# Placing each stage of the maxima and of the rest by table in a hand-ordered attention kernel

## What is computed

```python
# layer 0, per batch: attention over all 1024 tokens, 4 heads of 16
x_ln = layernorm(x) ; q, k, v = split(x_ln @ qkv_w)
attn = softmax(q k^T * scale) ; x = x + proj(attn v)
x = x + fc2(gelu(fc1(layernorm2(x))))
# layer 1, per batch: 8 heads of 64, each token sees the 32 tokens up to it
t = ln(tokens(x)) ; q, k, v = t Wq, t Wk, t Wv
t = tokens(x) + softmax_over_window(q . k_window) v_window @ Wu + bu
# then over all batches
Wx = ln(t) W ; Wx = batchnorm(Wx) ; y_t = sigmoid(Wx_t + y_{t-1} V^T)
result = t + y
```

## Time and profile before

| | us |
|---|---|
| three runs | 541.43, 546.31, 546.99 (median 546.31) |
| profiled execution | 541.36 |
| its span in the trace | 539.4 |
| PE busy | 461.1 |
| DVE busy | 328.0 |
| ACT busy | 291.6 |

### The profile page before, as it was taken

How to read it: one execution, slowest core, us unless ns; L and a number is a source line. 1 busy time by engine, 2 the same in 40 slices (tenths; PEclk the granted TensorE clock), 3 DMA queues, 4 the chain that set the end, 5 groups by cost and what they waited for, 6 DMA issues and landing times.

```text
span 539.4 us, 7934 instructions
## 1 busy us (share of the span) xinstructions
PE 461.1 (85%) x3257; PEld 178.3 (33%) x3257; DVE 328.0 (61%) x605; ACT 291.6 (54%) x499; POOL 12.9 (2%) x15
## 2 busy tenths in 40 slices
PE   7886889988989798787998987889998879995884
PEld 2442322222234332232233322222243323542583
DVE  3696868789748653689568654696332644514414
ACT  3442665755674365564873574648855655172242
POOL 9000000000000000000000000000000000000000
PEclk9896998989999999999999999999999998997897
DMA  8100180006300000017000000000000000000003
GB/s 295 28 1 2 41 136 1 1 1 121 56 2 1 1 1 1 1 33 144 0 2 1 1 1 2 0 0 1 2 2 1 1 0 1 2 1 1 1 1 79
DMA packets 6196, 13.09 MB, mean 24 GB/s; under 512 B 1296, under 2 KB 3600, under 8 KB 6032
## 3 DMA queue, kind: packets, MB, share of 16 engines
q1 hardware_dynamic: 6160, 12.58, 10.4%
HBM read 9.07 MB, written 3.41 MB: 23 GB/s over the span
## 4 chain that ended last, share of the span: by engine, by line
PE 66%; DVE 21%; ACT 8%; issue 3%; DMA 1%; SPq 1%; DVEq 0%; ACTq 0%
DVE part_max L1156 8%; PE O L725 8%; PE R L773 5%; PE T L690 4%; PE T L710 4%; PE R L621 3%; PE R L710 3%; PE R L882 3%; PE R L629 3%; PE R L690 3%; PE R L843 3%; PE R L870 2%; PE T L600 2%; PE R L857 2%; DVE zs L1267 2%
## 5 line engine op out<-in xcount | busy, mean ns | idle before, releaser
L1156 DVE TENSOR_REDUCE part_max<-T 128x1 f32<-128x512 f32 x170 | 112.0, 682 | 29.5 <-PE T L690 29.4
L1016 ACT ACTIVATE probs<-T 128x512 f32<-128x512 f32 x150 | 85.9, 597 | 41.2 <-PE T L710 41.0
L1016 ACT ACTIVATE probs<-R 128x512 f32<-128x512 f32 x106 | 62.0, 597 | 57.9 <-PE R L710 57.6
L690 PE MATMUL T<-KX,QX 96*128 96x512 bf16 x170 | 63.6, 395 | 9.7 <-DVE part_max L1156 8.3
L725 PE MATMUL O<-probs,VT 128*32 128x512 f32 x512 | 68.6, 611 | 1.1 <-ACT probs L1016 1.1
L1156 DVE TENSOR_REDUCE part_max<-R 128x1 f32<-128x512 f32 x86 | 57.4, 681 | 11.8 <-PE R L690 11.7
L710 PE MATMUL T<-QX,KX 99*128 99x512 bf16 x150 | 54.7, 389 | 7.5 <-DMA QX<-mx_part 5.5
L710 PE MATMUL R<-QX,KX 99*128 99x512 bf16 x106 | 40.3, 389 | 1.4 <-ACT probs L1016 0.7
L690 PE MATMUL R<-KX,QX 96*128 96x512 bf16 x86 | 33.2, 394 | 2.7 <-DVE part_max L1156 2.4
L773 PE MATMUL R<-xp,abd 128*128 128x512 f32 x64 | 32.3, 603 | 2.7 <-DVE xp L1125 2.6
L1040 ACT ACTIVATE p<-R 128x1024 f32<-128x1024 f32 x14 | 14.3, 1023 | 31.6 <-PE R L843 31.6
(11 more groups left out here) (220 smaller groups left out, 648.1 us busy)
## 6 DMA issues: line engine op xcount, KB each, us to landing
qk_scratch<-qk_part SPq DMA_DIRECT2D x6, 384.0 KB, 4.4
zs<-early SPq DMA_DIRECT2D x1, 2048.0 KB, 7.8
QX<-qk_scratch SPq DMA_DIRECT2D x3, 384.0 KB, 4.9
KX<-qk_scratch SPq DMA_DIRECT2D x3, 384.0 KB, 7.0
result<-probs SPq DMA_DIRECT2D x2, 512.0 KB, 5.1
s_rest<-rest SPq DMA_DIRECT2D x1, 882.0 KB, 10.1
X<-x SPq DMA_DIRECT2D x2, 384.0 KB, 11.9
QX<-qk_scratch SPq DMA_DIRECT2D x3, 256.0 KB, 7.7
```

The source lines that it names most:

```text
L690: mm(ring["max_piece", b, half, i], QX[b % 2][0:KQ, half, h, nt * P:(nt + 1) * P], KX[b % 2][0:KQ, kh, h, :], start=True, stop=True).then_ ...
L1016: A(probs[:, u % 2, h, :], ring["scores", b, u, h], ACT.Exp, scale=HD ** -0.5).then_inc(g["exp_done"], 1)
L1156: nc.vector.tensor_reduce(part_max[:, row, kh:kh + 1], ring["max_piece", b, half, i], AX_X, ALU.max).then_inc(g["max_red"], 1)
```

## The change

The weights, `merged`, `max_stages`, `ROOM` and `COST` go. In their place stand tables: for each stage of the maxima of a half (`MAX_AT`, seven tuples), for each stage of the projections and the rest (`LAYER_AT`), and for the end of the kernel (`END_AT`, `UNIFY_AT`), the number of main stages ahead of it. The main stages are the 64 scores and 16 values of each batch, 80 per batch, counted through from 0 to 319; entries of `LAYER_AT` are in quarters of a main stage. The tables differ from batch to batch. The set of stages is the same. Besides, the first layer norm of batch 2 waits for the last users of banks R0 and R1, and the ring leaves these two banks at that stage.

```diff
-def merged(main, other, start=0):
...
+MAX_AT = (
+    (
+        0, 0, 0, 0, 0, 2, 3, 3, 4, 5, 8, 10, 10, 10, 10, 13, 14, 17, 17, 18, 18, 18, 20, 21, 22, 23, 23, 23, 26, 29,
+        39),
...
+LAYER_AT = (
+    0, 0, 3, 5, 15, 16, 21, 320, 316, 318, 328, 334, 343, 346, 348, 353, 353, 371, 384, 402, 411, 413, 421, 424,
...
+    main = [x for b in range(B) for x in attend_stages(b)]
+    maxima = []
+    for n, places in enumerate(MAX_AT, 1):
+        b, half = divmod(n, 2)
+        pieces = [("max_piece", b, half, i) for i in range(MAX_EARLY if n == 1 else 0, PIECES)]
+        maxima += zip([*pieces, *max_end(b, half)], places)
+    layer = [*project_stages(1), ("masks",)]
+    for b in range(B - 1):
+        layer += [*(project_stages(b + 2) if b + 2 < B else []), *rest_stages(b)]
+    layer += window_stages(B - 1) + out_stages(B - 1, unify_parts(B - 1) - 1)
+
+    among, late = list(zip(layer, LAYER_AT)), len(LAYER_AT)
+    done = [0, 0]
+    for i, stage in enumerate([*main, None]):
+        for passed in range(4):
+            while done[1] < late and among[done[1]][1] <= 4 * i + passed:
+                out.append(among[done[1]][0])
+                done[1] += 1
+            while done[0] < len(maxima) and maxima[done[0]][1] <= i:
+                out.append(maxima[done[0]][0])
+                done[0] += 1
+                if passed < 3:
+                    break
+        if stage:
+            out.append(stage)
+    end = [*mlp_stages(B - 1), *layernorm_stages(B - 1, 3)]
+    unify = [*(("unify", B - 1, h, 0) for h in range(0, H1, 2)), *out_stages(B - 1, 0)]
+    return out + between(layer[late:], [(x, n - late) for x, n in zip(end, END_AT)], [(x, n - late) for x, n in zip(unify, UNIFY_AT)])
...
-                elif item == ("scores", 1, 0, 0):
+                elif item == ("ln_mean", 2, 1, 0):
                     shared = (*OWN, *LENT)
+                    norm_free.extend((owner[4], owner[5]))
...
-                    else:
-                        pe.wait_ge(g["exp_done"], UNITS * H0)
-                        pe.wait_ge(g["max_red"], 3 * PIECES)
-                        pe.wait_ge(g["mx_r"], 3)
+                    elif b == 2:
+                        for free in norm_free:
+                            pe.wait_ge(g[free[0]], free[1])
```

More of the change, by code:

```diff
@@ L92, in project_stages, with max_end @@
     return [*layernorm_stages(b, 1), ("project", b), ("split", b), ("project_v", b)]
[L95 to L100, removed]
+def max_end(b, half):
+    return [("max_neg", b, half), ("max_rows", b, half), ("max_parts", b, half)]
 def mlp_stages(b):
     return [("den", b), ("den_exp", b), ("o_norm", b, 0), ("o_norm", b, 1), ("proj", b), *layernorm_stages(b, 2), ("fc1", b), ("fc2", b)]
-def merged(main, other, start=0):
[L110 to L122, removed]
 UNIFY_CUT = 3
-MAX_UNITS = 7
 VALUES_AFTER = 4
 MAX_EARLY = 4
-FIRST_GAP = 3
-COST = {"scores": 1.71, "values": 1.77, "max_piece": 0.62}
 def unify_parts(b):
@@ L157, in window_stages @@
         out += [("blk_den", b, r), ("blk_pv", b, r), ("blk_out", b, r)]
[L158 to L163, removed]
+    return out + [("unify", b, h, unify_parts(b) - 1) for h in range(0, H1, 2)]
 def rest_stages(b):
@@ L173, in attend_stages @@
     out = []
-    for half in range(2):
-        if half == 0:
-            ahead = max_stages(b, 1, MAX_UNITS, 0 if b else MAX_EARLY)
-        else:
[L178 to L186, removed]
@@ L187, in attend_stages @@
-    return out + [("values", b, UNITS - 1)]
[L191 to L196, removed]
-RELAY_AT = 3
+    for u in range(UNITS):
+        for h in range(H0):
+            out.append(("scores", b, u, h))
+            if u and h + 1 == VALUES_AFTER:
+                out.append(("values", b, u - 1))
@@ new lines, in attend_stages @@
+    return out + [("values", b, UNITS - 1)]
+MAX_AT = (
+    (
+        0, 0, 0, 0, 0, 2, 3, 3, 4, 5, 8, 10, 10, 10, 10, 13, 14, 17, 17, 18, 18, 18, 20, 21, 22, 23, 23, 23, 26, 29,
+        39),
+    (
+        39, 39, 39, 39, 46, 46, 47, 50, 50, 52, 52, 52, 55, 56, 56, 56, 56, 60, 61, 63, 63, 63, 65, 67, 68, 68, 70,
+        70, 70, 72, 73, 76, 76, 79, 79),
+    (
+        80, 80, 80, 81, 82, 82, 82, 84, 84, 85, 85, 86, 86, 86, 88, 88, 88, 88, 89, 97, 100, 100, 100, 101, 102, 103,
+        104, 109, 109, 109, 112, 113, 116, 116, 116),
+    (
+        118, 118, 118, 119, 119, 119, 121, 121, 121, 123, 126, 127, 127, 132, 134, 134, 135, 135, 135, 139, 139, 139,
+        140, 140, 140, 140, 143, 143, 143, 143, 143, 143, 144, 144, 148),
+    (
+        154, 154, 155, 155, 158, 158, 159, 159, 159, 162, 162, 166, 166, 166, 167, 168, 168, 168, 176, 176, 183, 183,
+        183, 183, 183, 189, 189, 189, 189, 189, 192, 192, 195, 195, 195),
+    (
+        198, 198, 198, 199, 201, 201, 202, 202, 207, 210, 210, 212, 212, 213, 215, 216, 225, 225, 225, 225, 226, 226,
+        226, 226, 227, 227, 229, 230, 230, 230, 230, 232, 233, 234, 237),
+    (
+        241, 241, 241, 241, 242, 242, 242, 243, 243, 255, 255, 257, 257, 258, 258, 258, 258, 261, 262, 264, 265, 266,
+        266, 267, 268, 268, 269, 269, 271, 271, 271, 271, 272, 275, 278),
+)
@@ new lines, with between @@
+LAYER_AT = (
[10 rows of a table added]
+)
+END_AT = (
+    214, 216, 218, 218, 220, 221, 221, 222, 224, 227, 227, 228, 229, 231, 231,
+)
+UNIFY_AT = (
+    275, 275, 275, 275, 276, 277, 277, 278, 278,
+)
+RELAY_AT = 3
+def between(host, *others):
+    out, done = [], [0] * len(others)
+    for i in range(len(host) + 1):
+        for n, other in enumerate(others):
+            while done[n] < len(other) and other[done[n]][1] <= i:
+                out.append(other[done[n]][0])
+                done[n] += 1
+        out += host[i:i + 1]
+    return out
@@ L206, in order_of_stages @@
         out += [*pieces[:RELAY_AT], ("relay", 0, h + 1) if h + 1 < H0 else ("products",), *pieces[RELAY_AT:]]
[L207 to L227, removed]
+    out += [*max_end(0, 0), *(("max_piece", 0, 1, i) for i in range(MAX_EARLY))]
+    main = [x for b in range(B) for x in attend_stages(b)]
[4 more added lines that the diff above has]
+        maxima += zip([*pieces, *max_end(b, half)], places)
@@ L449, in build @@
         OWN, LENT = (0, 1, 2), (3, 6)
-        ring, ring_free, lent_free = {}, {}, {}
+        ring, ring_free, lent_free, norm_free = {}, {}, {}, []
         def plan_ring():
```

1 line of the change is left out of this document (removed), and 9 rows, old and new, of the table LAYER_AT.

## The result

The new kernel takes 499.7 us (median; 499.4 to 501.0) against 543.9 (540.6 to 547.0): a ratio of 0.918, 95% interval 0.913 to 0.923. The prediction had 526.5 and a range down to 514. The sign was right, and the gain, 44.2 us, is two and a half times the 17.4 of the sum.

The account below looks back on a forecast made before the run. The prediction took PE's work plus its waits for late inputs as the bound; terms -8.2, -6.7, -1.0, -2.0, -3.0 and +3.5 sum to -17.4, from 541.4 to 524.0 us, raised to 526.5 for run spread; range 514 to 540.

Parts of the forecast that it names:

- the holes of the long batches: Batches 1 and 2: PE's waits before late stages, counted hole by hole, change by -6.7 and -8.2 us.
- bare units: Units of four scores and a values stage alone: PE stands 0.5 us in each of seven more, +3.5 us.
- batch 1 at 110: Batch 1, from its first scores to those of batch 2, lasts some 110 us instead of 117.1.
- the grown hole before ln_mean 4: Batch 2: less PE work lies between unify and ln_mean 4, so the wait grows by 1.0 us to over 2.
- rival 4: Bunches of three to five pieces make PE wait for banks that DVE empties; slower, 550.5 us; chance 0.04.
- Rival 1: Waits of 0.5 us and less go too, 4 us more in each long batch: 516 us; chance 0.11.
- the trace has nine holes over 0.6 us: Batch 2: these holes, 10.4 us together or 11.9 start to start, are the waits that the change acts on.
- Unit 8 starts at 79.6 ... batch 1 begins near 109.0: Batch 0: DVE's reductions at 0.68 us set these times, against 81.5 and 108.5 before; -1.0 us net.
- Both holes go: Batch 2: the holes of 1.77 and 0.83 us around o_norm and proj close, -2.6 us.
- The tail, -3.0: Last scores to recurrence: earlier window stages -1.3, blk_pv and blk_den further apart -0.8, unify ahead of blk_den 3 -0.9 us.
- PE's holds ... are all still paid: Whole kernel: PE's, DVE's and ACT's work stays the same, so the change in time is the change in waiting.
- Before unify, -1.1: Batch 2: a values stage and max_rows come between, so the hole of 1.11 us before unify closes.

Follow-up runs that it names:

- e11: New kernel's order with separate banks for scores and pieces of the maxima, against the new kernel: 563.7 us, where the new kernel takes 499.7.
- e15: Old order of stages in the new kernel's ring, with separate banks for scores and pieces, against the kernel before: 576.1 us, where that takes 543.9.
- e17: New kernel's order, but banks last used by a piece of the maxima are taken later, against the new kernel: 557.7 us.
- e7: New kernel with four pieces of the maxima put back into the two bare units around o_norm in batches 1 to 3: 501.9 us against 499.7.
- e4: New order for maxima and rest, old order for the end of the list: 507.7 us, ratio 0.933 to the kernel before.
- e3: Old order up to the last values, new order for the end of the list, in the new ring: 538.6 us, ratio 0.990 to the kernel before.
- e6: New kernel with blk_den, blk_pv and blk_out 3 of batch 3 ahead of the first unify, as before the change: 504.3 us against 499.7.
- e19: New kernel with block 3 of batch 3 ahead of unify, plus idle matmuls in PE's waits before the first of the last two layer norms: 500.5 us.
- e20: New kernel with only ln_mean 4 of batch 1 moved behind the next values stage: 503.2 us (496.7 to 507.2).
- e18: New kernel with ln_mean 4 of batch 1 moved behind a values stage and blk_den 3 of batch 3 ahead of unify: 507.6 us.

## Why the prediction was right or wrong

Right: faster, and why PE was the place to look; that no work changes; the holes of the long batches one by one, but for unify's in batch 2 (the two long batches together lose 19.9 us of waits, forecast 14.9, bare units aside); batch 1 at 110; the grown hole before ln_mean 4; that bunches of pieces (rival 4) do no harm in this order. Rival 1, small waits go as well, at 516, was the nearest of the four. The argument against it, that these waits come from ACT and DVE, which keep their work, is what fell.

The mechanism, less waiting for the same work, was right. The steps that failed are sizes, and one term put at nothing:

1. **Waits at the ring.** The step "the trace has nine holes over 0.6 us" had of the ring only o_norm's holes and the DMA waits to go, about 6 us in all. Measured, the ring's waits fell from 41.7 to 24.1. The rest of them were single waits of 0.2 to 0.6 before pieces, 65 of them over 0.05 us before and 30 after where a piece takes over a piece's bank (22.4 and 8.7 us). The page had them in front of me, 10.7 us "<-DVE part_max" in the groups of L690. Runs e11, e15 and e17 show that this part comes of the order and the turn of the banks together.
2. **"So PE stands 0.5 in each" (bare units, +3.5).** I took PE's holds from start to start, but DVE's and ACT's from the recorded length. A further exponential costs 0.49, a further reduction 0.60. A bare unit takes 1.96 against PE's 1.88 and costs 0.1. Values stages, which wait for exponentials, fell from 8.8 to 5.0 instead.
3. **"Unit 8 starts at 79.6 ... batch 1 begins near 109.0."** The same mistake: 32 and 28 reductions at 0.60 instead of 0.68 are 5 us. Batch 1 began at 103.8. Part of batch 0's gain is the clock besides: from the first scores the trace before has 7.8 us at half clock in it (granted 0.94 in the earlier trace rows), the new one 0.5.
4. **"Both holes go", because no piece stands around o_norm.** They went, and e7 gives 1.3 to 2.1 us in each batch to that reason, somewhat less than the 2.6, 2.6 and 2.0 taken. What closes the rest no run shows.
5. **The tail, -3.0.** It lost 8.8. e4 against the new kernel gives 8.0, e3 5.3; of the 4.6 us that unify's place makes, 3.8 are clock (e6 against e19). "PE's holds ... are all still paid" took them at one price: the earlier trace rows had a granted clock of 0.93 in the tail and 0.94 in batch 0 in front of me, and I took no term for it.
6. **Before unify, -1.1.** It waits 1.6 in the new kernel too: it needs blk_out 3, which now stands behind max_rows in DVE's queue, and DVE waits there 0.98 us for PE's part of max_rows. The -1.1 came from PE's queue alone.

Open: which part of the fit decides at the ring. It's shown that it is order and turn together, and that one place of 0.2 to 1.2 us undoes it; no run shows a rule by which a table could be judged without running it. Open too is how much of the losses of the half tables, the shifts and the other rings the clock makes, for which there is only the estimate above. And e20's spread leaves open whether the hole before ln_mean 4 has a price.

## What to carry to other kernels

Read the granted clock of each stretch before taking all holds at one price. Take the hold of every engine from start to start, not only TensorE's: here the recorded lengths of DVE and ACT are 13% and 22% too long for a queue. When queues are strict and buffers are handed out by turns, a change of order is worth its late inputs (which can be read hole by hole, within 20% here in the long batches; in the tail the forecast of 3.0 met 8.8) plus what happens at the buffers, which can be as large again and of either sign; sum the short waits by group before calling the long ones the whole. Change such orders whole: each half of this one is slower than nothing.

## What the runs showed that I had not expected

- Two tables that win 36 us together lose 18 and 36 alone, and a shift of one by one main stage costs 60.
- Banks apart cost the new order 64 us and the old one 32, with waits for inputs unchanged to within 1.1 us.
- Moving one or two stages seems to change how steady the kernel is: four executions of the new kernel lie within 1.5 us, the six of e18 and the six of e20 within 10 each, and in both the longer ones have the lower granted clock.
